# Three generations of edge buckets, adjacency counts in four pieces, and a GpSimd memset in front of each placing write

## The chip, the cores and the metric

The kernel runs on one core of one Trainium2 chip. The metric is the device time of one execution in microseconds; lower is better. A run executes the whole program once, from the inputs in HBM to the output in HBM.

## What is computed

Four graph layers are applied in turn to 6250 nodes of 64 features, with 200000 edges that are sorted by their destination `dst`. Cut to what matters here:

```
h = relu(layernorm(x)); x = x + relu(segment_sum(H_all[src, rel] * a, dst))       # L0: a message per edge
h = relu(layernorm(x)); x = x + A @ relu(A @ h)                                   # L1: two sums over edges
h = relu(layernorm(x)); x = x + gcn4(h)                                           # L2: four more sums with the same A, dense layers between
h = relu(layernorm(x))
v_e = segment_sum(edge_attr_48, src) / max(segment_sum(1, src), 1)                # L3: means of 48 edge features by src
x = x + relu(relu([h, v_e, u] @ W1 + b1) @ W2 + b2) @ W3 + b3
```

`A[dst, src]` counts the edges between two nodes. L3 sums by `src`, for which the edges are not sorted.

## The kernel before

The program has four stages, and every engine has its own hand-written list of instructions; what orders them between engines is semaphores only. There is no scheduler.

**The loop.** The edges are walked in 391 groups of 16 destination nodes (`NG`). GpSimd (POOL) gathers the rows of a table for the messages, four indirect DMAs for a group (L712, 1564 in all), up to 13 groups ahead. VectorE (DVE) makes one-hot matrices (L1395, L1369), TensorE multiplies them into a strip of `A` (L1860, L1861) and sums the messages (L1865). ScalarE (ACT) turns the strip into bytes (`store_counts`, L801 and L802 into `count_stage`), measures an overflow (L804, L805), and stores it with a DMA (L808) to `adjacency` in HBM; it waits for that store to land before it fills the single staging buffer again (`counts_stored`). Even and odd source tiles lie apart, `HW` = 100 words in each of two rows. Beside this the DVE and TensorE work out, for each edge, its place in `l3_sorted`: the edge's bucket (49 buckets of 128 source nodes) and its rank in it. Edges come in blocks of 4096 (`SB`, 48 blocks and a rest), and the bucket of an edge has a place in one of `GENS` = 2 **generations**: blocks 0 to 41 (`FIRST` = 42) go to the first with room for 30 x 128 rows in a bucket, the rest to the second with room for 6 x 128 (`CAPC`).

**The placing writes.** An edge's 48 features are split into three bf16 parts that add up exactly, 146 values in a row, and an indirect DMA of GpSimd writes 128 such rows to their places, 32 DMAs for a block. Two early blocks are placed right behind the last gather (L720, 64 writes); the others follow in one straight list, three row buffers (`rows16`) in turn (L738, 1499 writes). Each block waits once, on `l3_split`, for ScalarE to have finished its rows. A block's rows are made in three **steps**, high, middle and low (`split_high`, `split_middle`, `split_low`; ACT copies at L870, L857, L858, L881, DVE subtractions at L1272); `split_high` waits until the buffer's block before has landed (`l3_moved`). `split_step` puts the steps in slots of the ACT and DVE lists by `step_slot`: 120 of 135 steps (`AGG_STEPS`) over the 156 slots of the six aggregations, 15 over the 49 buckets of the first generation's sums.

**Six aggregations** (`agg`) compute `A @ U`. Each walks the 391 groups in 13 parts of 32 groups (`NH`, `HG`) and loads a part in two halves of 1600 KB (`half`, L578), each into its own buffer, and TensorE multiplies 25 and 24 tiles of a half (`multiply`, L1948); a half is loaded again once its tiles are done (`half_mm`). Between aggregation 3 and 4, and between 5 and 6, stand a dense layer (L1993 to L2004) and the scaling of `U` (L1288 to L1305), with no steps in them.

**The sums of L3.** Behind the last aggregation, for each generation and bucket, SyncE loads the bucket (L616), DVE and ACT make one-hot matrices (`node_hots`: L1681 and ACT L995, L997 in the first generation, L1684 in the second), and TensorE sums (`node_sums`, L2066). The sums of a generation start once its blocks have landed. The final MLP runs between the buckets of the last generation, four buckets behind.

Helper: `ch.link(ins)` lets the instruction raise a semaphore of its own engine and has the next instruction of that engine wait for it.

## Time and profile before

| | us |
|---|---|
| median of 3 runs (lowest to highest) | 4442.24 (4441.61 to 4444.57) |
| the profiled execution | 4443.71 |
| its span in the profile | 4442.0 |
| granted TensorE clock, mean | 0.837 of full speed |

All durations in the rows below are of the profiled execution. Its own time is 1.7 us above its span, and 1.5 us above the median, so a sum made in the span is carried over by adding 1.7 us. The engine named PE is TensorE, DVE VectorE, ACT ScalarE, POOL GpSimd and SP SyncE; a "q" behind a name is that engine's sequencer, which issues DMAs and handles semaphores. The row of a POOL indirect DMA (DMA_INDIRECT) covers the making of its descriptors on GpSimd, not the movement of the data.

### The profile page before, as it was taken

What the parts mean: (1) busy time and instruction counts of PE and PEld (TensorE: products, weight loads), DVE (VectorE), ACT (ScalarE), POOL (GpSimd) and SP (SyncE); (2) the same over time, 40 slices, a digit from 0 to 9 for tenths busy, and PEclk for the clock granted to TensorE, in tenths of its full rate; (3) what the DMA queues carried; (4) which work ended last, traced back from release to release, by engine and by line L of the source; (5) the groups of instructions that cost most, each with busy time, mean ns of one, the idle gap of its engine ahead of it and who ended that gap; (6) DMA issues with size and microseconds to landing.
All of it is one profiled execution on the core that took longest, in us unless ns stands there. A gap on an engine that the chain in (4) does not pass through costs nothing.

```text
span 4442.0 us, 78060 instructions
## 1 busy us (share of the span) xinstructions
PE 2917.6 (66%) x18243; PEld 1666.8 (38%) x18244; DVE 2719.6 (61%) x9781; ACT 1518.2 (34%) x3741; POOL 3060.2 (69%) x3186
## 2 busy tenths in 40 slices
PE   4477777777777777777807676185685775672556
PEld 2144444444444444444403333032332333331544
DVE  5488888898988889888852221511413213218878
ACT  2234444444444444434412221122122121133881
POOL 2277777777777777777777777777567776577650
PEclk8699998898998999989858888597597885885779
DMA  5554444444444444444327766286086670673664
GB/s 180 155 128 104 109 103 101 108 105 103 106 110 100 104 109 108 102 105 109 72 89 235 241 207 219 68 267 200 20 266 201 208 254 26 207 227 134 236 216 116
DMA packets 599825, 650.57 MB, mean 146 GB/s; under 512 B 422854, under 2 KB 435892, under 8 KB 593429
## 3 DMA queue, kind: packets, MB, share of 16 engines
q1 hardware_dynamic: 382453, 463.07, 34.0%
q0 software_dynamic: 100064, 110.65, 12.2%
q10 hardware_dynamic: 117184, 75.50, 5.8%
q8 instruction: 41, 0.67, 0.1%
q14 instruction: 83, 0.68, 0.1%
HBM read 453.58 MB, written 192.06 MB: 145 GB/s over the span
## 4 chain that ended last, share of the span: by engine, by line
POOL 26%; issue 10%; DVE 6%; PE 5%; DMA 3%; ACT 1%; DVEq 0%; POOLq 0%; ACTq 0%; SPq 0%
POOL l_sorted L738 25%; POOL l_sorted L720 1%; DVE hid_T L1681 1%; DMA ld_all<-l_sorted 1%; PE bank L2066 1%; PE bank L1998 1%; PE bank L2004 1%; PE bank L1948 1%; DMA rel_and_z<-adjacency 1%; DVE hid_T L1684 0%; ACT work L947 0%; DVE G L1549 0%; DMA rel_and_z<-l_sorted 0%; DVE G L1585 0%; PE bank L2038 0%
## 5 line engine op out<-in xcount | busy, mean ns | idle before, releaser
L738 POOL DMA_INDIRECT l_sorted<-arena,l_pos x1499 | 1466.2, 978 | 585.3 <-issue 454.6
L712 POOL DMA_INDIRECT ld_all<-rel_table,rel_and_z x1564 | 1493.5, 955 | 507.4 <-issue 409.6
L1860 PE MATMUL bank<-hid_T 128*128 128x400 f16 x2346 | 852.4, 364 | 494.6 <-DVE arena L1404 415.6
L1861 PE MATMUL bank<-hid_T 128*128 128x384 f16 x2346 | 835.3, 356 | 0.0
L1395 DVE TENSOR_SCALAR hid_T<-count_key,hid_T 128x400 f16<-128x400 int16 x2346 | 624.5, 334 | 17.0 <-PE bank L1865 10.6
L1948 PE MATMUL bank<-ld_all 128*128 128x512 fp8e4 (+1 forms) x1950 | 465.2, 401 | 186.4 <-DMA ld_all<-adjacency 113.2
L801 ACT CAST ld_all<-bank 128x400 fp8e4<-128x400 f32 x391 | 192.3, 492 | 1072.6 <-DMA adjacency<-ld_all 798.0
L1860 PEld LDWEIGHTS bank<-hid_T 128*128 x2346 | 240.0, 102 | 733.6 <-issue 579.6
L1948 PE MATMUL bank<-rel_and_z,ld_all 128*128 128x512 fp8e4 (+1 forms) x1872 | 417.5, 382 | 92.4 <-DMA rel_and_z<-adjacency 92.3
L1865 PE MATMUL bank<-ld_all,arena 128*32 x4692 | 428.7, 233 | 0.0
L1865 PEld LDWEIGHTS bank<-ld_all,arena 128*32 128x32 f32 x4692 | 319.7, 113 | 172.1 <-issue 127.9
L1369 DVE TENSOR_SCALAR hid_T<-io,arena 128x256 f16<-128x256 f16 x1564 | 360.3, 304 | 0.1
L1321 DVE COPY accT<-bank 128x512 f32<-128x512 f32 (+1 forms) x78 | 51.2, 656 | 503.8 <-PE bank L1948 503.8
L1948 PEld LDWEIGHTS bank<-ld_all 128*128 128x128 f16 x1950 | 194.7, 106 | 433.1 <-issue 270.0
L1948 PEld LDWEIGHTS bank<-rel_and_z,ld_all 128*128 128x128 f16 x1872 | 179.4, 101 | 326.4 <-issue 147.8
L1861 PEld LDWEIGHTS bank<-hid_T 128*128 x2346 | 241.9, 103 | 136.0 <-issue 52.1
L916 ACT COPY G<-bank 128x256 f32<-128x256 f32 (+1 forms) x78 | 27.9, 358 | 623.8 <-PE bank L1957 622.2
L2066 PE MATMUL bank<-ld_all,hid_T 128*128 128x145 bf16 x1188 | 117.3, 270 | 185.3 <-ACT hid_T L997 87.9
L804 ACT ACTIVATE ld_all<-bank,minus_max 128x400 f16<-128x400 f32 x391 | 238.2, 609 | 0.0
L805 ACT ACTIVATE ld_all<-bank,minus_max 128x384 f16<-128x384 f32 x391 | 231.1, 591 | 0.0
L802 ACT CAST ld_all<-bank 128x384 fp8e4<-128x384 f32 x391 | 189.6, 485 | 0.0
L1272 DVE TENSOR_TENSOR src_f<-src_f,bank 128x512 f32<-128x512 f32 x96 | 60.2, 682 | 211.4 <-ACT arena L858 211.3
(309 smaller groups left out, 4233.6 us busy)
## 6 DMA issues: line engine op xcount, KB each, us to landing
ld_all<-adjacency SPq DMA_DIRECT2D x72, 1600.0 KB
rel_and_z<-adjacency SPq DMA_DIRECT2D x72, 1600.0 KB, 9.5
l_sorted<-zeros SPq DMA_DIRECT2D x151, 424.0 KB
arena<-in_edge_attr SPq DMA_DIRECT2D x195, 256.0 KB
adjacency<-ld_all ACTq DMA_DIRECT2D x391, 100.0 KB
ld_all<-l_sorted SPq DMA_DIRECT2D x33, 1095.0 KB, 6.6
rel_table<-ld_all SPq DMA_DIRECT2D x49, 520.0 KB, 3.6
ld_all<-rel_table,rel_and_z POOLq DMA_INDIRECT x1564
```

The source lines that it names most:

```text
L712: pool.indirect_dma_start(ring[:, c % RING, 0:TW], None, rel_table, bass.IndirectOffsetOnAxis(ap=rel_i[:, c:c + 1], axis=0)).then_inc(s(f" ...
L738: pool.indirect_dma_start(l3_sorted, bass.IndirectOffsetOnAxis(ap=l3_pos[0:parts, n * SB_K + k:n * SB_K + k + 1], axis=0), rows16[q][0:par ...
L801: act.copy(count_stage[:, 0:w0], b0[:, 0:w0], saturate=False)
L802: act.copy(count_stage[:, w0:GW], b1[:, 0:GW - w0], saturate=False)
L804: act.activation(over_junk[:, 0:w0], b0[:, 0:w0], ACT.Relu, bias=minus_max[:], accum_out=over[:, bass.ds(g * 2, 1)])
L805: act.activation(over_junk[:, w0:GW], b1[:, 0:GW - w0], ACT.Relu, bias=minus_max[:], accum_out=over[:, bass.ds(g * 2 + 1, 1)]).then_inc(s( ...
L1369: v.tensor_scalar(lo_ring[:, q * K + k, :], io256[:], lo_in[:, k0 + k:k0 + k + 1], None, ALU.is_equal)
L1395: v.tensor_scalar(pair_hot[q % 2][:, k, :], count_key[:], pair_in[q % 2][:, k:k + 1], None, ALU.is_equal)
L1860: pe.matmul(b0[:, 0:w0], low[:, 0:P], pair_hot[q % 2][:, k, 0:w0], start=k == 0, stop=k == CG - 1)
L1861: pe.matmul(b1[:, 0:GW - w0], low[:, P:2 * P], pair_hot[q % 2][:, k, 0:GW - w0], start=k == 0, stop=k == CG - 1)
L1865: ins = pe.matmul(half_sums[q // 4][:, q % 4 * TW:(q % 4 + 1) * TW], weights[q % 2][:, k, :], ring[:, bass.ds((first64 + k) % RING, 1), 1: ...
L1948: ins = pe.matmul(bank[slot][:, 0:n * GN].rearrange("p (g d) -> p g d", d=GN), x16[:, t, :], a_half[side][:, 0:n, t // 2 * GN:(t // 2 + 1) ...
```

## The change

**Generations.** `GENS` becomes 3: blocks 0 to 35, 36 to 43 and the rest, with room for 26, 7 and 4 x 128 rows in a bucket. `l3_first` and `leave` become arrays over the generations that are past. The 135 steps are spread anew: 102 over the aggregations, 25 over the sums of generation 0, 8 over those of generation 1 (`STAGE_STEPS`), none in the last. The room for sorted rows grows from 36 to 37 x 128 rows a bucket, so 157 DMAs clear it instead of 152.

**Counts in four pieces.** A group's strip is stored as four rows of `QW` = 52 words (13 tiles, the last a tile short) instead of two of 100, so a store has 512 runs of 208 bytes instead of 256 runs of 400 bytes. In the aggregations each half is loaded as two pieces of 832 KB with a buffer and a semaphore of its own, and is asked for again once the 13 or 12 tiles of that piece are done. The order of tiles (even, then odd) and the number of matmuls stay. TensorE waits per piece.

**The memset.** Behind the loop, each of the 1499 placing writes gets a linked memset of 128 x 16 float32 in front: it clears a corner of `w_rel`, which nothing reads at that time, and the DMA waits for it. The two early blocks and the gathers have none.

**Small things.** `starts` is loaded into the buffer where it is used, one memset less; two semaphore pairs of paths that this input doesn't take become one; `packed_ready` is counted on `setup`.

```diff
-GENS = 2
-CAPC = (30, 6)
-FIRST = 42
-AGG_STEPS = 120
+GEN_END = (36, 44, NSB + 1)
+GENS = 3
+CAPC = (26, 7, 4)
+AGG_STEPS = 102
+STAGE_STEPS = (25, 8)
-HW = HI * GN // 4
+QT = -(-HI // 2)
+QW = QT * GN // 4
+PIECE_TILES = [(side, u0, min(u0 + QT, HI - side)) for side in range(2) for u0 in (0, QT)]
...
     for k in range(SB_K if n < NSB else REST_DMAS):
         parts = REST_TAIL if n == NSB and k == REST_K else P
+        ch.link(pool.memset(w_rel[:, 0:1, 0:16], 0))
         pool.indirect_dma_start(l3_sorted, bass.IndirectOffsetOnAxis(ap=l3_pos[0:parts, n * SB_K + k:n * SB_K + k + 1], axis=0),
                                 rows16[q][0:parts, k, :], None).then_inc(s(f"l3_moved{q}"), 16)
...
-                act.dma_start(adjacency_row[:, bass.ds(b, 1), q, :, :], count_words.rearrange("p (a o f) -> p a o f", a=1, o=2)).then_inc(s("counts_stored"), 16)
+                act.dma_start(adjacency_row[:, m, c, q, :, :], count_words.rearrange("p (a o f) -> p a o f", a=1, o=4)).then_inc(s("counts_stored"), 16)
...
-                        link(v.scalar_tensor_tensor(l3_first[:], held_out, leave[:, bass.ds(n, 1)], l3_first[:], ALU.mult, ALU.add))
+                        for g in range(GENS - 1):
+                            past = v.scalar_tensor_tensor(l3_past[:, g, :], held_out, leave[:, g, bass.ds(n, 1)], l3_past[:, g, :], ALU.mult, ALU.add)
+                        link(past)
...
-                    coming = [(m, side, 2 * (NH * a + m) + side + 1) for m in range(0 if a == 0 else 1, NH) for side in range(2)]
+                    coming = [(m, i, 4 * (NH * a + m) + i + 1) for m in range(0 if a == 0 else 1, NH) for i in range(4)]
...
-                        for side in range(2):
-                            pe.wait_ge(s(f"half_in{side}"), loads)
+                        for i, (side, u0, u1) in enumerate(PIECE_TILES):
+                            pe.wait_ge(s(f"piece_in{i}"), loads)
```

GpSimd at the start of the placing writes of the first block behind the loop, before (L738 is the write):

```order
L726 TENSOR_LOAD flags [waits flag2_ready]
L726 ISA x2
L727 COMPARE_AND_BRANCH
L738 DMA l_sorted<-arena,l_pos 242176x146 [waits l3_moved0,l3_pos_ready,l3_split]
L738 DMA l_sorted<-arena,l_pos 242176x146 x31
```

and of the changed kernel (L743 is the memset, L744 the write):

```order
L731 TENSOR_LOAD flags [waits flag2_ready]
L731 ISA x2
L732 COMPARE_AND_BRANCH
L743 MEMSET w_rel 128x16 [waits l3_moved0,l3_pos_ready,l3_split]
L744 DMA l_sorted<-arena,l_pos 248448x146 [waits pool_chain]
L743 MEMSET w_rel 128x16
L744 DMA l_sorted<-arena,l_pos 248448x146 [waits pool_chain]
```

The block's wait moved to the memset, and each write, which followed its predecessor with no wait of its own, now waits for the memset in front of it.

ScalarE in the sums of the first generation, before; L995 and L997 are the one-hot matrices of a bucket, L857, L858, L881 and L886 are parts of steps:

```order
L995 ACTIVATE hid_T<-io,node_key 128x128 x8
L997 ACTIVATE hid_T<-hid_T,ones 128x1152 [waits act_chain]
L857 CAST bank<-src_f 128x512 [waits split_less]
L857 CAST bank<-src_f 128x512 x2
L858 COPY arena<-src_f 128x32x48
L995 ACTIVATE hid_T<-io,node_key 128x128 [waits node_key,node_mm]
L995 ACTIVATE hid_T<-io,node_key 128x128 x8
L997 ACTIVATE hid_T<-hid_T,ones 128x1152 [waits act_chain]
L995 ACTIVATE hid_T<-io,node_key 128x128 [waits node_key,node_mm]
L995 ACTIVATE hid_T<-io,node_key 128x128 x8
L997 ACTIVATE hid_T<-hid_T,ones 128x1152 [waits act_chain]
```

and of the changed kernel at the same place:

```order
L1002 ACTIVATE hid_T<-io,node_key 128x128 x8
L1004 ACTIVATE hid_T<-hid_T,ones 128x1152 [waits act_chain]
L864 CAST bank<-src_f 128x512 [waits split_less]
L864 CAST bank<-src_f 128x512 x2
L865 COPY arena<-src_f 128x32x48
L1002 ACTIVATE hid_T<-io,node_key 128x128 [waits node_key,node_mm]
L1002 ACTIVATE hid_T<-io,node_key 128x128 x8
L1004 ACTIVATE hid_T<-hid_T,ones 128x1152 [waits act_chain]
L888 COPY arena<-src_f 128x32x48 [waits split_less]
L893 DMA src_f<-in_edge_attr 128x1536 [waits l3_split]
```

The low step (L881, now L888) that finishes a block stood three buckets behind the middle one; now it stands one bucket behind it.

## Rows read from the trace of the kernel before

**Rows 1.** The page's head and its first part, the busy time of each engine.

```profile
span 4442.0 us, 78060 instructions
PE 2917.6 (66%) x18243; PEld 1666.8 (38%) x18244; DVE 2719.6 (61%) x9781; ACT 1518.2 (34%) x3741; POOL 3060.2 (69%) x3186
```

**Rows 2.** GpSimd in order of time: start, duration, instruction, idle before it, releaser.

```profile
201.95 1.15 POOL L712 DMA_INDIRECT ld_all<-rel_table,rel_and_z  x1 [3.38 <-issue]
...
2198.56 0.95 POOL L712 DMA_INDIRECT ld_all<-rel_table,rel_and_z  x1 [0.30 <-issue]
...
2281.82 0.97 POOL L720 DMA_INDIRECT l_sorted<-ld_all,l_pos  x1 [0.30 <-issue]
2283.10 0.96 POOL L738 DMA_INDIRECT l_sorted<-arena,l_pos  x1 [0.30 <-issue]
...
4333.40 0.90 POOL L738 DMA_INDIRECT l_sorted<-arena,l_pos  x1 [0.30 <-issue]
```

**Rows 3.** GpSimd's waits behind the loop, 2283 to 4340 us: total, times, longest.

```profile
POOL l_sorted L738 <- issue: 454.6, 1491, 0.5
POOL l_sorted L738 <- ACT arena L881: 130.7, 8, 44.1
```

**Rows 4.** GpSimd in order of time: writes that wait between aggregations and in the sums.

```profile
3229.53 0.96 POOL L738 DMA_INDIRECT l_sorted<-arena,l_pos  x1 [44.13 <-ACT arena L881]
...
3799.84 0.96 POOL L738 DMA_INDIRECT l_sorted<-arena,l_pos  x1 [36.70 <-ACT arena L881]
...
4300.06 0.97 POOL L738 DMA_INDIRECT l_sorted<-arena,l_pos  x1 [13.14 <-ACT arena L881]
```

**Rows 5.** GpSimd in order of time, in setup: linked instructions one behind the other.

```profile
2.43 0.20 POOL L641 MEMSET ones<- 128x128 f32 x1
2.70 0.10 POOL L642 MEMSET minus_max<- 128x1 f32 x1
2.86 0.47 POOL L643 IOTA count_key<- 128x400 int16 x1
```

**Rows 6.** The same view: two memsets without links, and one form beside VectorE.

```profile
0.32 0.10 POOL L2103 MEMSET const-float32-0.0<- 128x1 f32 x1 [0.32 <-issue]
0.35 0.10 POOL L2103 MEMSET const-float32-1.0<- 128x1 f32 x1
...
35.52 0.94 POOL L688 MEMSET h<- 128x16 bf16 x1 [28.24 <-DMA h<-in_edge_attr]
...
65.03 0.17 POOL L688 MEMSET h<- 128x16 bf16 x1 [19.95 <-DMA h<-in_edge_attr]
```

**Rows 7.** ScalarE in order of time: the copy that releases the write at 4300.06 (rows 4).

```profile
4297.77 1.47 ACT L881 COPY arena<-dst_f 128x1536 bf16<-128x1536 bf16 x1 [1.48 <-DVE dst_f L1272]
```

**Rows 8.** Busy time of PE, PEld, DVE, ACT and POOL, 2283 to 4337 us.

```profile
2283.00:4337.00 2054.00, 1223.96 (x6264) 663.18 (x6264) 729.92 (x2344) 601.58 (x1085) 1466.17 (x1499) 0.78 0.58 188
```

**Rows 9.** VectorE's groups in the sums of generation 0, 4070 to 4300 us.

```profile
L1693 DVE TENSOR_REDUCE U<-bank 128x48 f32<-128x144 f32 x42 | 12.7, 303 | 31.3 <-PE bank L2066 31.3
```

**Rows 10.** The tail, 4337 to 4442 us: busy times, then VectorE's first groups.

```profile
4337.00:4442.00 105.00, 72.03 (x493) 46.18 (x493) 90.18 (x250) 21.00 (x39) 0.00 (x0) 0.92 0.49 120
L1684 DVE TENSOR_TENSOR hid_T<-io,ld_all 128x768 bf16<-128x768 f16 x33 | 31.3, 950 | 11.9 <-DMA ld_all<-l_sorted 11.8
L1684 DVE TENSOR_TENSOR hid_T<-io,rel_and_z 128x768 bf16<-128x768 f16 x16 | 15.2, 950 | 0.0
```

**Rows 11.** TensorE's groups, 2330 to 4005 us: count, busy us, mean ns, idle before.

```profile
L1948 PE MATMUL bank<-ld_all 128*128 128x512 fp8e4 (+1 forms) x1950 | 465.2, 401 | 186.4 <-DMA ld_all<-adjacency 113.2 <-DVEq L1306 73.2
L1948 PE MATMUL bank<-rel_and_z,ld_all 128*128 128x512 fp8e4 (+1 forms) x1872 | 417.5, 382 | 92.4 <-DMA rel_and_z<-adjacency 92.3
```

**Rows 12.** ScalarE in order of time, in the loop: a strip's cast and its store.

```profile
1018.24 0.38 ACTq L808 DMA_DIRECT2D adjacency<-ld_all  x1
1020.24 0.49 ACT L801 CAST ld_all<-bank 128x400 fp8e4<-128x400 f32 x1 [2.16 <-DMA adjacency<-ld_all]
1022.43 0.38 ACTq L808 DMA_DIRECT2D adjacency<-ld_all  x1
```

More of the change, by code:

```diff
@@ L259, in step_slot @@
                 return step * (2 * NH * 6) // AGG_STEPS
-            return 2 * NH * 6 + (step - AGG_STEPS) * NBK // (split_steps - AGG_STEPS)
+            step, slot = step - AGG_STEPS, 2 * NH * 6
+            for n in STAGE_STEPS:
+                if step < n:
+                    return slot + step * NBK // n
+                step, slot = step - n, slot + NBK
         step_at = {step_slot(step): step for step in range(split_steps)}
-        assert AGG_STEPS % 3 == 0 and len(step_at) == split_steps and FIRST <= AGG_STEPS // 3 + EARLY
+        assert AGG_STEPS % 3 == 0 and len(step_at) == split_steps == AGG_STEPS + sum(STAGE_STEPS) and len(STAGE_STEPS) == GENS - 1
+        assert all(GEN_END[g] <= (AGG_STEPS + sum(STAGE_STEPS[0:g])) // 3 + EARLY for g in range(GENS - 1))
         n_cols = (NSB + 1) * SB_K
@@ L998, in _ @@
                     split_step(2 * NH * 6 + t, (0, 1, 2))
-                act.wait_ge(s("node_hot"), NBK + 1)
+                for t in range((GENS - 2) * NBK):
+                    split_step(2 * NH * 6 + NBK + t, (0, 1, 2))
+                act.wait_ge(s("node_hot"), (GENS - 1) * NBK + 1)
                 for t in range(NBK):
@@ L1044, in _ @@
             link(v.memset(eps[:], EPS))
[L1045 to L1046 removed]
+            for g in range(GENS - 1):
+                v.memset(stay[:, GEN_END[g] - 1:GEN_END[g]], 0)
+                v.memset(leave[:, g, GEN_END[g] - 1:GEN_END[g]], 1.0)
             v.memset(s12[:, SRC_T:NT, :], 0)
@@ L1167, in _ @@
             link(v.tensor_scalar(l3_bucket, low_f, 1.0 / P, None, ALU.mult))
-            link(v.tensor_scalar(l3_pos[:, 0:FIRST * SB_K], l3_bucket[:, 0:FIRST * SB_K], float(CAP[0]), None, ALU.mult))
-            link(v.tensor_scalar(l3_pos[:, FIRST * SB_K:n_cols], l3_bucket[:, FIRST * SB_K:n_cols], float(CAP[1]), float(NBK * CAP[0]), ALU.mult, ALU.add))
+            for g in range(GENS):
+                of_gen = slice(((0,) + GEN_END)[g] * SB_K, GEN_END[g] * SB_K)
+                link(v.tensor_scalar(l3_pos[:, of_gen], l3_bucket[:, of_gen], float(CAP[g]), float(NBK * sum(CAP[0:g])), ALU.mult, ALU.add))
             v.wait_ge(s("setup_mm"), 2)
@@ L1347, in _ @@
                 chains.append(fast)
-                link(v.memset(digits[:, NG:WORDS * PACK], 0))
-                link(v.tensor_copy(digits[:, 0:NG], starts[0:1, 0:NG]))
+                link(v.tensor_copy(digits, starts))
                 link(v.scalar_tensor_tensor(digits[:, 0:NG], minus_base[0:1, :], float(K) / GN, digits[:, 0:NG], ALU.mult, ALU.add))
@@ L1434, in positions @@
                     v.tensor_tensor(l3_pos[:, cols], l3_pos[:, cols], l3_rank[:], ALU.add).then_inc(s("l3_pos_ready"), 1)
-                link(v.memset(count_words[:, GW // 4:2 * HW], 0))
+                link(v.memset(count_words, 0))
                 v.wait_ge(s("setup_mm"), 3)
@@ L2068, in node_sums @@
                     ins.then_inc(s("node_mm"), 1)
+                for n in range((GENS - 1) * NBK):
+                    node_sums(n // NBK, n)
                 for t in range(NBK):
-                    node_sums(0, t)
-                for t in range(NBK):
-                    node_sums(1, NBK + t)
+                    node_sums(GENS - 1, (GENS - 1) * NBK + t)
                     b = t // BT - 1
```

122 lines of the change are left out of this document (61 added, 61 removed).

## The prediction

> **What bounds the kernel now.** I first looked for the engine that never rests. The page's busy shares don't name it: GpSimd is busiest with 69%, TensorE has 66%, VectorE 61% [rows 1]. GpSimd in order of time does. Its gathers run from 201.95 to 2198.56 us, 1564 of them, one every 1996.6 / 1563 = 1.277 us, with an idle time of 0.30 us between two; the early writes follow at the same pace, and the 1499 later ones start at 2283.10 and end at 4333.40 + 0.90 = 4334.3 us [rows 2]. The gap of 0.30 is put down to "issue", that is, to no other engine. Behind the loop GpSimd waits for others only 8 times, 130.7 us in all, always for the copy that finishes a block's rows [rows 3]. So the time is 2283.1, plus 1498 starts at a pace, plus 130.7 of waits, plus a tail from 4334.3 to 4442.0, which is 107.7. The pace is (4333.40 - 2283.10 - 130.7) / 1498 = **1.281 us a write**.
>
> Two of the waits, 44.1 and 36.7, lie in the dense layers, where no steps stand; the other six, 130.7 - 80.8 = 49.9 us, lie in the sums of generation 0 [rows 3, 4]. At a dense layer GpSimd has two finished blocks, 64 writes or 82 us, and needs the third after 82 + 44.1 = 126.1 us, at the other layer after 118.7.
>
> **The memset.** It stands on this engine 1499 times, and each write waits for it. I call what it adds to the pace m. No row shows a write behind a memset, so I bound m by three neighbours.
>
> In setup, linked instructions stand one behind the other: 128x128 at 2.43, the next at 2.70, the next at 2.86. A linked memset thus costs its own 0.20 or 0.10 and 0.06 to 0.07 for the link [rows 5]. For 16 columns I take 0.10 + 0.10 x 15/127 = 0.11, with the link **m = 0.18**. It counts once if the write's gap of 0.30 stays as it is.
>
> The floor is no cost: two memsets without a link start 0.03 us apart [rows 6], and if the memset ran inside the gap of 0.30, m would be 0.
>
> The ceiling is a write that starts from rest. The copy that releases the write at 4300.06 ends at 4297.77 + 1.47 = 4299.24, so from permission to start pass 0.82 us [rows 4, 7], not 0.30. Part of these 0.82 is hidden today under the write before. If a write that waits for its memset has to go through all of it, the gap is 0.07 + 0.11 + 0.82 = 1.00 instead of 0.30, and m = 0.70. In that row, however, the engine's sequencer stood in front of a semaphore instruction with the write behind it not yet taken in, whereas now the memset and the write can both be taken in while the previous write runs. That, and that a link costs 0.06 in setup, is why I take the low neighbour.
>
> The Trainium skill's page "Perfetto Trace Analysis", section "DMA Instruction — SWDGE (GPSIMD)", has such an instruction decoded and pushed into a wait queue before its semaphores are looked at. That speaks for 0.18, and no row here shows it for a waiting write.
>
> m applies 1498 times and is partly given back at the dense layers, since two blocks then last 64m longer: waits there become 80.8 - 128 x 0.18 = 57.8. Net 1498 x 0.18 - 23.0 = **+246.6 us**.
>
> **What the memset meets on VectorE.** One form of memset takes 0.17 us at one time and 0.94 at another [rows 6]. The Trainium skill's page "SBUF — State Buffer", section "SBUF: two separate sides", says that GpSimd is locked out of a shared port pair while VectorE runs certain instructions; if every VectorE instruction did that, the sum would be the third rival's. The writes argue against much of it: 1466.17 / 1499 = 0.978 us on average with VectorE busy for 729.92 of 2054 us [rows 8], against 0.96 or 0.97 undisturbed [rows 2]. I add nothing.
>
> **Three generations, the steps.** In the sums of generation 0 the steps came too slowly: 42 buckets in 230 us are 5.5 us each [rows 9], three steps of 15 in 49 slots are 9.8 buckets or 54 us for a block, against 32 x 1.281 = 41 us of writes. With 25 steps it is 5.9 buckets or 32 us, and a block of writes lasts 32 x 1.461 = 47. GpSimd isn't starved there any more: **-49.9 us**. In generation 1, 8 steps in 49 slots are 18.4 buckets for a block, by the tail's 105 / 49 = 2.1 us [rows 10] 39 us, still under 47. In the aggregations 3 steps of 102 in 156 slots are 4.6 slots for a block; TensorE's matmuls and their waits for loads make (465.2 + 417.5 + 113.2 + 92.3) / 156 = 7.0 us a slot [rows 11], 32 us a block, under 47 too. Where steps stand next to the dense layers the tables agree: the last step before is in slot 76, the next in 78 and 79, in both kernels, so these two waits stay but for m.
>
> **The tail.** Once the last write lands, only the last generation is left. VectorE is busy for 90.2 of 105 us there, with one hot instruction of 0.950 us for 6 tiles in each of 49 buckets [rows 10]. With 4 tiles two thirds stay, about 0.65: 49 x 0.3 = **-15 us**. Generations 0 and 1 are done by then: generation 1 may start 4 blocks and a rest before the end, over 155 writes or 226 us, and needs about 49 x 2.1 = 103.
>
> **Counts in four pieces: nothing.** TensorE's matmuls wait 113.2 + 92.3 us for adjacency loads between 2330 and 4005 [rows 11], and smaller pieces should take much of that away. But the aggregations are paced by GpSimd: every step waits for a landed block, and TensorE, faster, waits longer for the copies between. What was saved goes into waiting for steps.
>
> In the loop the store gets 512 runs instead of 256. ScalarE's round is 2.19 us from cast to store and 2.00 from store to the next cast, 4.19 in all [rows 12], against 4 x 1.277 = 5.11 for GpSimd's four gathers, the cover that hides it. The added part is between 0 and 2.00, a doubling; 0.92 fit. I take 0 on the path. One VectorE instruction more for 8 groups, about 0.2 us in 41, and five more clearing DMAs are under the same cover; a memset less at `starts` is worth 0.
>
> **Sum.** 4443.7 + 246.6 - 49.9 - 15 = **4625 us**, of the profiled execution's own time, which stands 1.5 above the median. By pieces: 2283.1 + 1498 x 1.461 + 0.9 + 57.8 + 92.7 + 1.7. It is 4.1% slower. The other edits are worth 64.9 together, so the memset decides the sign: at m = 64.9 / 1370 = 0.047 us it comes out even.
>
> **Rivals.**
> - *The memset is free* (m about 0): it runs in the 0.30 us gap, which may be the wait of descriptor making alone. Then 4443.7 - 64.9 = **4379 us**, faster by 1.5%. For it: the gap is always 0.30 whatever stands around, and unlinked memsets cost 0.03. Against it: the change makes the write wait for the memset's end, and links cost 0.06 to 0.07 beside the memset itself. It decides below m = 0.047.
> - *Each write starts from rest* (m = 0.70): 2283.1 + 1498 x 1.981 + 0.9 + 92.7 + 1.7, with no wait left at the dense layers since 64 x 1.981 is above 126: **5346 us**. For it: the only row of a write that starts after a wait shows 0.82. Against it: the sequencer's reading ahead.
> - *VectorE holds up the memset*: 0.94 - 0.17 = 0.77 more in 36% of cases, m = 0.46: 2283.1 + 1498 x 1.741 + 0.9 + 22 + 92.7 + 1.7 = **5008 us**. Against it: the 0.978 above.
> - *The store becomes the loop's bound*: a doubling of 2.00 makes ScalarE's round 6.19, 391 x 1.08 = +422 us: **5047**. It decides once the store adds 0.92. For it: one buffer only, and ScalarE waits for nearly every store. Against it: the store's start and landing don't scale with its runs.
>
> **Chances.** The sum 0.44 (m from 0.1 to 0.35); from rest 0.22; VectorE or something between 0.10; the store 0.06; free 0.14; about even 0.04. The likeliest gives 4625. Leaving out only the cases of m below 0.1, the range is **4560 to 5350**, 0.82 of the chances; the likeliest case alone would span 4560 to 4800. A measurement of this kernel tells about 0.2% from no change. Faster by more 0.14, within 0.03, slower by more 0.83.
>
> **What the profile after would show.** Rows of a 128x16 memset of about 0.11 us between writes, and starts of writes 1.46 us apart (1.28 if it is free, 1.98 if each starts from rest). The first of them still at 2283 us; later if the store binds, with ScalarE's wait behind a store over 2.9 us. Two waits of some 34 and 25 us for the low step's copy and none in the sums. Waits of TensorE for adjacency much shorter, and no gain from it. A tail of 93 us behind GpSimd's last write. The forecast is wrong if writes are paced differently, or if GpSimd waits for more than two blocks.

## The result, and the profile after

| | us |
|---|---|
| predicted | 4625 (range 4560 to 5350) |
| changed kernel, median of 4 runs (lowest to highest) | 4581.18 (4573.49 to 4595.54) |
| kernel before, median of 4 runs beside it | 4442.95 (4441.61 to 4444.57) |
| ratio after to before, 95% interval | 1.0309 (1.0297 to 1.0321) |
| the profiled execution of the changed kernel, and its span | 4575.16, 4573.4 |

The changed kernel is 3.1% slower. The forecast had the side and, within 1%, the time; several terms of its sum are off, partly against each other. The sections below take these terms one by one.

In the changed kernel L743 is the memset, L744 the placing write, L888 the low step's copy (L881 before). The head of the page, its busy times, and four of its costliest groups (line, engine, operation, names, shapes, count; busy us, mean ns of one; idle time before it and what ended most of it):

```profile
span 4573.4 us, 80273 instructions
PE 2895.2 (63%) x18292; PEld 1684.2 (37%) x18293; DVE 2766.6 (60%) x9833; ACT 1517.8 (33%) x3741; POOL 3268.7 (71%) x4685
...
L744 POOL DMA_INDIRECT l_sorted<-arena,l_pos x1499 | 1483.3, 990 | 439.9 <-POOL w_rel L743 410.4
...
L1962 PE MATMUL bank<-ld_all 128*128 128x512 fp8e4 (+1 forms) x1950 | 435.7, 384 | 76.3 <-DVEq L1317 74.1
...
L1962 PE MATMUL bank<-rel_and_z,ld_all 128*128 128x512 fp8e4 (+1 forms) x1872 | 394.2, 367 | 1.7 <-DMA rel_and_z<-adjacency 1.7
...
L743 POOL MEMSET w_rel<- 128x16 f32 x1499 | 190.6, 127 | 64.9 <-ACT arena L888 63.5
```

GpSimd is busy 208.5 us longer than in [rows 1], 190.6 of them memsets. TensorE's waits for adjacency loads, 113.2 and 92.3 us in [rows 11], are all but gone, 1.7 in the second group, and no time came of it.

GpSimd in order of time (start, duration, instruction, idle before it and releaser), at the same place as [rows 2], then at a waiting write as [rows 4], then beside VectorE in the sums of generation 1, and its last write:

```profile
2484.97 0.98 POOL L744 DMA_INDIRECT l_sorted<-arena,l_pos  x1 [0.28 <-POOL w_rel L743]
2485.94 0.12 POOL L743 MEMSET w_rel<- 128x16 f32 x1
2486.35 0.97 POOL L744 DMA_INDIRECT l_sorted<-arena,l_pos  x1 [0.28 <-POOL w_rel L743]
2487.32 0.12 POOL L743 MEMSET w_rel<- 128x16 f32 x1
2488.71 0.97 POOL L744 DMA_INDIRECT l_sorted<-arena,l_pos  x1 [1.26 <-issue]
...
3170.11 0.11 POOL L743 MEMSET w_rel<- 128x16 f32 x1 [34.62 <-ACT arena L888]
3170.80 0.97 POOL L744 DMA_INDIRECT l_sorted<-arena,l_pos  x1 [0.58 <-POOL w_rel L743]
...
4264.69 1.18 POOL L744 DMA_INDIRECT l_sorted<-arena,l_pos  x1 [0.28 <-POOL w_rel L743]
4265.88 0.12 POOL L743 MEMSET w_rel<- 128x16 f32 x1
4266.28 1.19 POOL L744 DMA_INDIRECT l_sorted<-arena,l_pos  x1 [0.28 <-POOL w_rel L743]
...
4462.90 0.91 POOL L744 DMA_INDIRECT l_sorted<-arena,l_pos  x1 [0.28 <-POOL w_rel L743]
```

Three things are to be seen. The memset starts the moment the write before it ends, and the write follows 0.28 us behind the memset, not 0.30: writes start **1.38 us apart**, not 1.46. One write, that at 2488.71, starts 1.26 us behind its memset instead of 0.28, and I call such a write late. And at 4265 a write takes 1.18 us instead of 0.97.

GpSimd's waits behind the loop, 2283 to 4600 us (total, times, longest), against [rows 3]:

```profile
POOL l_sorted L744 <- POOL w_rel L743: 410.4, 1476, 0.6
POOL w_rel L743 <- ACT arena L888: 63.5, 2, 34.6
POOL l_sorted L744 <- issue: 29.4, 23, 1.6
```

The two waits are those at the dense layers, 34.6 and 28.9; in the sums there is none. The last line is the late write of above: 23 times a write starts about 1 us late. These are the 50th write behind the loop, with a gap of 1.64 us, and from the 146th (the one at 2488.71) to the 1490th every 64th, each with 1.26.

The tail, from the end of the last write at 4463.8 (the columns are stretch, its length, busy time of PE, PEld, DVE, ACT and POOL, granted TensorE clock, DMA share, GB/s), with the stretch ahead of it, and two of VectorE's groups:

```profile
4370.00:4464.00 94.00, 1.61 (x12) 1.04 (x10) 1.65 (x5) 0.00 (x0) 74.17 (x135) 0.50 0.09 27
4464.00:4573.00 109.00, 73.97 (x395) 45.13 (x395) 78.08 (x251) 20.99 (x39) 0.00 (x0) 0.81 0.32 83
...
L1696 DVE TENSOR_TENSOR hid_T<-io,ld_all 128x512 bf16<-128x512 f16 x32 | 21.8, 683 | 0.0
...
L1708 DVE TENSOR_REDUCE hid_T<-bank 128x48 f32<-128x144 f32 x50 | 15.1, 303 | 8.8 <-PE bank L2081 8.8
```

Against [rows 10] VectorE has 12 us less to do (78.1 for 90.2), as forecast, its hot instruction takes 0.68 us for 0.95. But the tail is 4573.4 - 4463.8 = 109.6 us, where it was 107.7. TensorE has fewer matmuls (395 for 493) and is busy longer (74.0 for 72.0), because its granted clock is 0.81 where it was 0.92, and VectorE now waits for it 8.8 us at one line where [rows 10] had it busy for 86% of the tail.

### The profile page after: what moved, and what is told of

It reads as the page before. It is cut to its first block, busy times and chain, and to the rows that moved or that the text cites. A ratio compares the mean times of both kernels' runs of the same rounds, so it can differ in the third digit from the quotient of the medians.

```text
span 4573.4 us, 80273 instructions
## 1 busy us (share of the span) xinstructions
PE 2895.2 (63%) x18292; PEld 1684.2 (37%) x18293; DVE 2766.6 (60%) x9833; ACT 1517.8 (33%) x3741; POOL 3268.7 (71%) x4685
## 4 chain that ended last, share of the span: by engine, by line
POOL 35%; issue 9%; PE 4%; DVE 2%; ACT 1%; DMA 0%; DVEq 0%; POOLq 0%; ACTq 0%; SPq 0%
POOL l_sorted L744 30%; POOL w_rel L743 4%; POOL l_sorted L725 1%; PE bank L2013 1%; PE bank L2019 1%; ACT work L954 0%; PE bank L2059 0%; PE bank L2067 0%; PE bank L2053 0%; PE bank L1962 0%; DVE work L1299 0%; DVE hid_T L1696 0%; DVE work L1621 0%; DVE G L1561 0%; DVE G L1597 0%
## 5 line engine op out<-in xcount | busy, mean ns | idle before, releaser
L744 POOL DMA_INDIRECT l_sorted<-arena,l_pos x1499 | 1483.3, 990 | 439.9 <-POOL w_rel L743 410.4
L1962 PE MATMUL bank<-ld_all 128*128 128x512 fp8e4 (+1 forms) x1950 | 435.7, 384 | 76.3 <-DVEq L1317 74.1
L1962 PE MATMUL bank<-rel_and_z,ld_all 128*128 128x512 fp8e4 (+1 forms) x1872 | 394.2, 367 | 1.7 <-DMA rel_and_z<-adjacency 1.7
L2081 PE MATMUL bank<-ld_all,hid_T 128*128 128x145 bf16 x1217 | 139.6, 290 | 260.7 <-issue 118.3
L1962 PEld LDWEIGHTS bank<-ld_all 128*128 128x128 f16 x1950 | 193.2, 104 | 293.2 <-issue 110.8
L743 POOL MEMSET w_rel<- 128x16 f32 x1499 | 190.6, 127 | 64.9 <-ACT arena L888 63.5
L1972 PE MATMUL bank<-work,accT 128*128 128x64 f32 x588 | 86.6, 296 | 234.9 <-DVE accT L1332 234.9
L2081 PEld LDWEIGHTS bank<-ld_all,hid_T 128*128 128x128 bf16 x1217 | 119.9, 128 | 287.9 <-issue 287.7
```

The costliest lines, as they stand in the source:

```text
L743: ch.link(pool.memset(w_rel[:, 0:1, 0:16], 0))
L744: pool.indirect_dma_start(l3_sorted, bass.IndirectOffsetOnAxis(ap=l3_pos[0:parts, n * SB_K + k:n * SB_K + k + 1], axis=0), rows16[q][0:par ...
L1962: ins = pe.matmul(bank[slot][:, 0:n * GN].rearrange("p (g d) -> p g d", d=GN), x16[:, 2 * u + side, :], a_piece[i][:, 0:n, (u - u0) * GN:( ...
L2081: ins = pe.matmul(bank[n % 3][:, 0:KEY], node_hot[n % 2][:, k, :], sorted_in[n % 3][:, k, 0:KEY], start=k == 0, stop=k == CAPC[gen] - 1)
```

## Experiments

Each starts from the kernel that its text names and changes what the text says; the kernel before ran beside each on the same chip. A ratio is always to the kernel before. In the texts of what was expected, "hots" are one-hot matrices.

### The changed kernel without its memsets

```diff
-                        ch.link(pool.memset(w_rel[:, 0:1, 0:16], 0))
```

> The changed kernel with the 1499 memsets taken out; three generations, steps and four pieces stay. Theory A (the memset costs its own 0.12 us on the engine that bounds, the rest of the change is a gain): pace of the writes back to 1.28 us, no stall every 64 writes, no write waits in the sums; with start at 2284, two dense waits of 44 and 37 us and a tail of 93 to 108 us the time is 4380 to 4398 us. Rival B (the other edits gain nothing, because the matrices of generation 1 now hold up the writes beside them and the tail is no shorter): 4425 to 4445 us.

Measured: 4427.08 us (4419.31 to 4439.38), ratio 0.9960 (0.9946 to 0.9974). This is in rival B's range: all the other edits together win some 17 us of the median, not the 64.9 of the forecast. In its profiled execution (span 4437.6) the first write is at 2285.60, and GpSimd's last one ends at 4309.3, 25.0 us before that of the kernel before. The waits in the sums are gone, as forecast:

```profile
POOL l_sorted L743 <- issue: 455.4, 1494, 0.3
POOL l_sorted L743 <- ACT arena L887: 81.1, 5, 43.5
```

but the writes are 1.296 us apart in the mean, (4308.35 - 2285.60 - 81.1) / 1498, against 1.281, which is 22 us, and the tail is 4437.6 - 4309.3 = 128.3 us, 20.6 more than before. So two losses stand against what was to be gained, and neither comes from the memset. The experiments with tiles and with added matmuls take them up.

### The kernel before, with the memset alone

```diff
+                        ch.link(pool.memset(w_rel[:, 0:1, 0:16], 0))
                         pool.indirect_dma_start(l3_sorted, ...
```

> The kernel before with the linked memset in front of each of the 1499 later writes, nothing else. Theory A: pace 1.27 + 0.11 = 1.38 us undisturbed, 1498 x 0.11 = +165, 24 stalls of 1 us every 64 writes +24, given back 14 at the dense layers and about 18 in the sums of generation 0: 4443 + 157 = about 4600 us. Rival B (the memset's price depends on the three generations or the pieces, through VectorE): pace under 1.33 us undisturbed and under 4540 us.

Measured: 4585.62 us (4581.40 to 4587.57), ratio 1.0315 (1.0298 to 1.0333): as slow as the whole change. First and last write start at 2283.82 and 4474.10, and the waits for the copy are

```profile
POOL w_rel L738 <- ACT arena L882: 89.7, 6, 34.3
POOL l_sorted L739 <- issue: 29.4, 23, 1.6
```

so a write has (4474.10 - 2283.82 - 89.7) / 1498 = 1.402 us, 0.121 more than before. Of the 181 us that the memsets add, 41 are given back by shorter waits (130.7 to 89.7), 9 more than theory A said, which is most of why the time is below its 4600. The price hardly depends on the generations, 0.121 us a write with two and 1.411 - 1.296 = 0.115 with three, and the 23 late writes are there too, the same ones by number.

### A satisfied wait in place of the memset

```diff
-                        ch.link(pool.memset(w_rel[:, 0:1, 0:16], 0))
+                        pool.wait_ge(s("l3_split"), m + 1)
```

> The changed kernel with no memsets; instead each write waits on a semaphore that has long been reached. It separates the wait as such from the memset. If the stall every 64 writes comes from waits that keep the sequencer from reading ahead, it shows here too, every 64 or 128 writes. If a wait as such costs pace, the pace is over 1.30. Theory A: pace 1.28 us, no stalls, the time of the kernel without memsets within 10 us.

Measured (one run): 4424.59 us; 1.27 us from write to write in the median, 1.297 in the mean of the unbroken ones, as without memsets. A wait in front of each write that was satisfied long ago costs nothing that this run shows, and no write is late by 1 us.

### The memset kept, but the write doesn't wait for it

```diff
-                        ch.link(pool.memset(w_rel[:, 0:1, 0:16], 0))
+                        pool.wait_ge(ch.sem, ch.base + ch.k)
+                        ch.also(pool.memset(w_rel[:, 0:1, 0:16], 0))
```

Each memset waits for the memset before it, which is long done, and the write for nothing.

> The changed kernel with the same 1499 memsets, but the writes don't wait for them: only the next memset waits for the one before, which is long done. It separates the memset's own time from the link. Theory A (GpSimd's time of the memset counts, and the gap of 0.28 before a write is the write's own): pace 1.38 us as with the link, within 0.02. Rival: the link is what costs, and without it the memset goes into the gap: pace 1.28 to 1.31 us and the time near that of the kernel without memsets. The stall every 64 writes: gone if the waiting write keeps the sequencer from reading ahead, there if it goes by the count of instructions.

Measured (one run): 4448.19 us, 133 us less than the changed kernel. GpSimd in order of time:

```profile
2486.12 0.97 POOL L745 DMA_INDIRECT l_sorted<-arena,l_pos  x1 [0.18 <-issue]
2487.09 0.13 POOL L744 MEMSET w_rel<- 128x16 f32 x1
2487.40 0.98 POOL L745 DMA_INDIRECT l_sorted<-arena,l_pos  x1 [0.18 <-issue]
```

The same memsets stand there, just as long, and the writes start 1.28 us apart. The gap behind the write before is 0.13 + 0.18 = 0.31 us: the memset runs inside it. It isn't wholly free: over all writes the pace is (4318.87 - 2284.58 - 78.8) / 1498 = 1.305 us against 1.296 without memsets, some 14 us for 1499 of them, where the waited-for memset costs 172. So the gap isn't idle time that GpSimd needs behind a memset; it is a stretch of about 0.30 us behind the last write in which a memset is all but free, unless the next write waits for the memset. Then most of it, 0.28, begins anew at the memset's end. **The wait costs, not the work.** The late writes are absent here too.

### Two linked memsets

```diff
                         ch.link(pool.memset(w_rel[:, 0:1, 0:16], 0))
+                        ch.link(pool.memset(w_rel[:, 0:1, 16:32], 0))
```

> The changed kernel with a second linked memset of 128x16 ahead of each write. The forecast's own term, a linked memset costs its duration and a link of 0.06 us: the starts of writes go from 1.38 to some 1.56 us apart, no wait left at the dense layers that is longer than 25 us, time 4800 to 4850. Rival, only the first one is cheap and the second waits for the first from rest: 1.7 us or more, over 5000. On the delay of about 1 us that the changed kernel has at every 64th write: if it goes by instructions on GpSimd (every 128th), it comes at every 42nd or 43rd write now, some 35 times; if by writes, at every 64th as before, 23 times.

Measured: 4848.98 us, ratio 1.0904 (1.0883 to 1.0926).

```profile
2614.07 0.12 POOL L743 MEMSET w_rel<- 128x16 f32 x1
2614.25 0.11 POOL L744 MEMSET w_rel<- 128x16 f32 x1
2614.64 0.97 POOL L745 DMA_INDIRECT l_sorted<-arena,l_pos  x1 [0.28 <-POOL w_rel L744]
...
2617.16 0.12 POOL L743 MEMSET w_rel<- 128x16 f32 x1
2617.35 0.11 POOL L744 MEMSET w_rel<- 128x16 f32 x1
2618.72 0.97 POOL L745 DMA_INDIRECT l_sorted<-arena,l_pos  x1 [1.26 <-issue]
```

The second memset adds 0.17 us (1.55 between writes in the median), which is a memset and its link as in setup [rows 5]: 0.18 and 0.19 from memset to memset here. The first adds 0.10. So the forecast's 0.18 is right for a memset that stands behind a memset and too high for one that takes part of a write's gap. The late writes are still the 50th, 146th, 210th and so on: they go by writes, not by instructions, of which there are half as many again. What they wait for isn't settled. They appear only where a write waits for a memset of its own engine, in five of five such kernels, and in none of the others.

### The counts in four pieces alone

```diff
-GEN_END = (36, 44, NSB + 1)
-GENS = 3
-CAPC = (26, 7, 4)
-AGG_STEPS = 102
-STAGE_STEPS = (25, 8)
+GEN_END = (42, NSB + 1)
+GENS = 2
+CAPC = (30, 6)
+AGG_STEPS = 120
+STAGE_STEPS = (15,)
-                        ch.link(pool.memset(w_rel[:, 0:1, 0:16], 0))
```

> The kernel before with the counts in four pieces alone (two generations, 120 and 15 steps, no memset). The forecast's step, no worth on the path: 4443 within 5 us, although TensorE's waits for adjacency loads (113.2 + 92.3 us before) fall below 100. Rival, the gain reaches the path or the doubled runs of the store cost something: under 4430, or the first placing write later than 2286 us and the time over 4455.

Measured: 4444.93 us (4442.21 to 4450.08), ratio 0.9996 (0.9987 to 1.0005). The adjacency waits of [rows 11] vanish here as well:

```profile
L1961 PE MATMUL bank<-ld_all 128*128 128x512 fp8e4 (+1 forms) x1950 | 444.0, 389 | 74.5 <-DVEq L1316 72.9 <-DMA ld_all<-adjacency 1.6
L1961 PE MATMUL bank<-rel_and_z,ld_all 128*128 128x512 fp8e4 (+1 forms) x1872 | 395.5, 369 | 0.9 <-DMA rel_and_z<-adjacency 0.9
```

205 us of waiting on an engine that doesn't set the pace were worth nothing, and the store's doubled runs cost nothing on the path: the first write is at 2281.93. The store itself did get longer. Between 400 and 2190 us ScalarE's waits for it are 859.7 us for 321 here and 836.9 for 317 in the changed kernel, against 714.8 for 296 before, so one is 2.68, 2.64 and 2.41 us. The 0.2 to 0.3 us that it grew by are well under the 0.92 of the prediction.

### Generation 1's one-hot matrices in tiles, no memsets

On the kernel without memsets, generation 1's one-hot matrices are made as generation 0's are, a copy of the keys and one VectorE instruction for each 128x128 tile, instead of one instruction of 128x896.

```diff
-                    if gen == 0:
+                    if gen < GENS - 1:
...
-                        for k in range(CAPC[0] - ACT_HOTS):
+                        for k in range(CAPC[0] - ACT_HOTS if gen == 0 else CAPC[gen]):
```

> The changed kernel without its memsets, and generation 1's hot columns made by 7 instructions of 128x128 a bucket, as generation 0's are, instead of one of 128x896. Theory E, the one wide VectorE instruction is what stretches GpSimd's writes there (75 writes in 116 us instead of 91): the writes keep 1.28 us, the last one lands 15 to 20 us earlier, time some 4405 to 4412. Rival F, the writes are stretched by something else that runs in those 116 us (loads of 112 KB a bucket, the sums, any VectorE work): no more than 5 us are won, time 4420 to 4430.

Measured: 4414.64 us (4409.76 to 4418.47), ratio 0.9931 (0.9918 to 0.9945), by the ratios some 13 us less than without this edit. The median is 3 us above theory E's range and 5 below rival F's, so the time alone doesn't decide; the trace does. The groups of GpSimd and VectorE in generation 1's sums, first without the edit (4107 to 4223 us), then with it (4103 to 4225 us):

```profile
L743 POOL DMA_INDIRECT l_sorted<-arena,l_pos x75 | 93.6, 1249 | 22.9 <-issue 22.9
L1695 DVE TENSOR_TENSOR hid_T<-io,ld_all 128x896 bf16<-128x896 f16 x32 | 34.8, 1086 | 2.0 <-DMA ld_all<-l_sorted 1.5
L1695 DVE TENSOR_TENSOR hid_T<-io,rel_and_z 128x896 bf16<-128x896 f16 x16 | 17.4, 1087 | 2.0 <-DMA rel_and_z<-l_sorted 1.8
```

```profile
L743 POOL DMA_INDIRECT l_sorted<-arena,l_pos x96 | 93.3, 972 | 29.3 <-issue 29.3
L1692 DVE TENSOR_SCALAR hid_T<-io,node_key 128x128 bf16<-128x128 f16 x360 | 64.3, 277 | 1.8
```

VectorE has more to do with the tiles (64.3 us for 52.2), and yet the writes are back at 0.97 us, 96 of them in 122 us instead of 75 in 116. It is the wide instruction that stretches GpSimd's writes, up to 1.84 us for one. The kernel before ran this instruction only behind GpSimd's last write; the third generation put 49 of them beside it. The last write ends at 4286.5 for 4309.3; 20 of these 22.8 us are the pace.

Whether the form or the length of 1.09 us does it can be read from the trace of the kernel before, which has other VectorE instructions beside GpSimd's writes:

```profile
3726.33 0.69 DVE L1609 TENSOR_TENSOR work<-work,hid_T 128x512 f32<-128x512 f32 x1 [2.27 <-ACT work L947]
3726.43 1.43 POOL L738 DMA_INDIRECT l_sorted<-arena,l_pos  x1 [0.31 <-issue]
...
2860.00 5.39 DVE L1288 TENSOR_REDUCE work<-U 128x64 f32<-128x3136 f32 x1
2861.95 0.97 POOL L738 DMA_INDIRECT l_sorted<-arena,l_pos  x1 [0.30 <-issue]
```

An instruction of 0.69 us with two inputs in SBUF goes with a write of 1.43 us (the copy L1600, which follows it, leaves writes at 0.97 where it runs alone), and one of 5.39 us with a single input leaves the write at 0.97. The subtractions L1272 take 0.68 us and have two inputs too, but one of them lies in PSUM (`bank`): the writes beside them alone stay at 0.96 and 0.97, 154 of 154. Two-input instructions of 128x256 (0.42 us) go with writes of up to 1.23. So it isn't the length that decides; all 27 writes of over 1.10 us behind the loop stand beside a TENSOR_TENSOR whose two inputs both lie in SBUF. The rule isn't sharp: L1609 left other writes at 0.97, and beside one-input instructions of 128x256 writes took mostly 1.03 and once 1.10.

The Trainium skill's page "SBUF — State Buffer", section "SBUF: two separate sides", has a VectorE instruction with two SBUF inputs hold a port pair against GpSimd instructions that read SBUF, whichever of the two starts first, and the other fully blocked meanwhile. The direction fits: the 128x896 form reads two tensors, the tile form one and a column of keys, and the memset, which reads none, stays at 0.12 us beside it (0.125 in the mean of 77 in the changed kernel). The writes of that stretch are 0.28 us longer in the mean and 0.87 at most; no row shows the whole 1.09.

### TensorE kept busy ahead of the tail

On the kernel without memsets 640, on the changed kernel 760 added matmuls between the sums of generation 1 and those of the last generation, into a bank that nothing reads.

```diff
+                with pe.Fori(0, 80) as i:
+                    for k in range(8):
+                        pe.matmul(bank[7][:, 0:256], ident16[:], io256[:], start=True, stop=True)
                 for t in range(NBK):
                     node_sums(GENS - 1, (GENS - 1) * NBK + t)
```

> The changed kernel without its memsets, with 640 matmuls of 128x256 into an unused bank between the sums of generation 1 and those of the last (dummy work; results are the same). Theory C, the tail behind the last write is long because TensorE stands idle before it and then works at a granted clock of 0.5 to 0.6: the tail's clock comes to over 0.9, the tail falls from 128 us to 92 to 98, the time to 4392 to 4405. Rival D, the tail is set by VectorE, loads and the round between engines: the tail stays over 110 us whatever the clock, time 4415 to 4430.

> The changed kernel as it is, with 760 matmuls of 128x256 into an unused bank between the sums of generation 1 and those of the last. Theory C: the tail's clock goes from 0.81 to over 0.9, the tail from 109.6 to 92 to 98 us, the time to 4564 to 4570. Rival D: the tail stays at 107 to 110, time 4578 to 4585.

Measured: 4434.30 us (4427.87 to 4442.44), ratio 0.9973 (0.9962 to 0.9983), and 4593.10 us (4590.36 to 4599.50), ratio 1.0332 (1.0316 to 1.0348). Nothing is won; by the ratios 6 and 10 us are lost, but the intervals overlap with those without the added work. All the times of both theories were missed: 4434.30 is above rival D's 4430, 4593.10 above its 4585, and the changed kernel's tail became 126.3 us. The stretch of the added matmuls and the tail, for the kernel without memsets, and the end of that stretch by itself:

```profile
4223.00:4309.00 86.00, 69.86 (x632) 62.01 (x630) 0.77 (x2) 0.05 (x1) 62.32 (x65) 0.92 0.11 33
4309.00:4433.00 124.00, 100.18 (x395) 59.96 (x395) 78.01 (x250) 20.95 (x39) 0.00 (x0) 0.58 0.26 69
...
4280.00:4293.00 13.00, 12.86 (x118) 11.28 (x116) 0.00 (x0) 0.00 (x0) 9.95 (x11) 1.00 0.11 32
4293.00:4309.00 16.00, 0.00 (x0) 0.01 (x1) 0.77 (x2) 0.05 (x1) 9.08 (x10) 0.61 0.17 50
```

The added matmuls end at 4292.9, 12 us before the last write, and TensorE then stands idle for 16 us until the tail's first matmul at 4309.0. The clock was at 1.00 in their last 13 us, fell in that pause, and was at 0.58 over the tail. So this run doesn't answer theory C as it stands, since the full clock was lost before the tail began; work that runs into the tail without a pause wasn't tried. It shows that the added work ahead buys nothing if a pause of 16 us follows. The next experiment decides from the other side.

### Added matmuls inside the tail

On the kernel with tiles and no memsets, 2 and then 5 added matmuls behind each of the last generation's 49 sums.

```diff
                     ins.then_inc(s("node_mm"), 1)
+                    if gen == GENS - 1:
+                        for k in range(2):
+                            pe.matmul(bank[7][:, 0:256], ident16[:], io256[:], start=True, stop=True)
```

> The kernel of the run with generation 1's hots in tiles (no memsets), and behind each of the last generation's 49 sums 2 matmuls of 128x256 into an unused bank (dummy work; results are the same), so that TensorE has as many matmuls a bucket there as the kernel before. Theory G, the clock in the tail is low because TensorE's work in the tail itself became thinner with 4 tiles instead of 6: the granted clock rises from 0.64 to 0.9 or more, the tail falls from about 121.5 us to 95 to 105, the time to 4390 to 4402. Rival H, the density inside the tail doesn't matter: the clock stays between 0.5 and 0.8, 98 matmuls of 0.11 to 0.28 us come on top, the time is 4415 to 4440.

> As the run with 2 dummy matmuls a bucket in the tail, with 5 of them. Theory G: the clock is 0.95 or more through most of the tail, tail 95 to 105 us (5 x 49 matmuls of 0.11 us are 27 us, of which most lies in TensorE's idle time), time 4388 to 4402. Rival H: clock between 0.5 and 0.8 and 245 matmuls of 0.22 to 0.28 us on top, tail over 150 us, time over 4440.

Measured: 4390.18 us (4389.29 to 4392.47), ratio 0.9874 (0.9858 to 0.9891), and 4391.01 us (4390.63 to 4391.66), ratio 0.9875 (0.9858 to 0.9891). The tails without added matmuls, with 2, and with 5, and below the first two their first 40 us:

```profile
4287.00:4408.00 121.00, 90.51 (x395) 54.62 (x395) 78.48 (x251) 21.01 (x39) 0.00 (x0) 0.66 0.29 75
...
4287.00:4307.00 20.00, 12.42 (x54) 7.73 (x55) 13.05 (x43) 2.38 (x5) 0.00 (x0) 0.50 0.30 84
4307.00:4327.00 20.00, 17.88 (x66) 10.82 (x65) 12.75 (x41) 3.33 (x6) 0.00 (x0) 0.50 0.28 74
```

```profile
4286.00:4387.00 101.00, 74.95 (x493) 46.17 (x493) 77.93 (x251) 21.00 (x39) 0.00 (x0) 0.94 0.34 90
...
4286.00:4306.00 20.00, 12.95 (x82) 7.70 (x83) 15.51 (x51) 2.38 (x5) 0.00 (x0) 0.78 0.39 105
4306.00:4326.00 20.00, 16.46 (x119) 10.56 (x117) 17.17 (x58) 5.00 (x9) 0.00 (x0) 1.00 0.35 92
```

```profile
4286.00:4389.00 103.00, 89.63 (x640) 61.40 (x640) 78.09 (x251) 21.00 (x39) 0.40 (x1) 0.93 0.34 88
```

With 98 matmuls more TensorE is busy for 15.6 us less, and the kernel 24 us faster. Both kernels come to the tail with an idle TensorE and a clock of 0.50 in the 20 us before it; the one with more matmuls is at the full clock 20 us later, the other still at 0.50. So what keeps the clock low is how little TensorE does inside the tail, and not the pause ahead of it. The third generation thus had two effects on the tail: less work for VectorE, and for TensorE too, 395 matmuls instead of 493, with which it no longer held the full clock of 2.4 GHz but fell for much of the tail to the 1.2 of the other level. All tails side by side, by the profiled executions:

| kernel | matmuls in the tail | granted clock | tail, us |
|---|---|---|---|
| before | 493 | 0.91 | 107.7 |
| counts in four pieces alone | 493 | 0.87 | 110.5 |
| before with the memset | 493 | 0.87 | 110.8 |
| changed | 395 | 0.81 | 109.6 |
| satisfied wait, no memset | 395 | 0.69 | 118.9 |
| tiles, no memset | 395 | 0.66 | 121.5 |
| changed, TensorE busy ahead | 395 | 0.61 | 126.3 |
| memset not waited for | 395 | 0.59 | 126.6 |
| no memset | 395 | 0.58 | 128.3 |
| no memset, TensorE busy ahead | 395 | 0.58 | 128.5 |
| two linked memsets | 395 | 0.55 | 131.7 |
| tiles and 2 added | 493 | 0.94 | 101.7 |
| tiles and 5 added | 640 | 0.93 | 102.6 |
| changed, with tiles and 2 added | 493 | 0.94 | 102.3 |

Within each count of matmuls the tail follows the clock, and only the ones with more matmuls have a high one every time. The changed kernel's four runs spread over 22 us and the five without memsets over 20, where those with 2 or 5 matmuls added in the tail lie within 5. That this spread is the tail's clock is likely and not shown. Only the clock of the whole span is on record for every run: without memsets it is highest, 0.823, in the fastest run and lowest, 0.815, in the slowest, but in the changed kernel it doesn't order them (0.810 at 4575.16, 0.811 at 4595.54). The Trainium skill's page "TensorE: Matmul & The Clock Gate", section "Part 1: The HAM clock gate (the "warmup" mystery)", has the clock follow how busy the array has been of late, and puts the cost of the ramp below 1% for a typical kernel. The direction is as in these tails; here the clock was worth 20 us of 4410, 0.5%, and 16% of a tail of 121.5.

### The changed kernel with tiles and 2 added matmuls

The two edits of above on the changed kernel, memsets and all.

> The changed kernel with its memsets, with generation 1's hots in tiles and 2 dummy matmuls behind each of the last generation's sums. If the losses simply add up: 4463.8 for the end of the last write, less about 12.5 writes x 1.38 = 17 us that the wide hots cost in generation 1's sums, plus a tail of 101.7 and 1.7 around the span, is 4550 us, within 6. The tail's granted clock is over 0.9. Rival, the memset hides what the two mends win (GpSimd's writes stay stretched beside 7 narrow instructions a bucket, now that a memset stands between them): 4565 or more.

Measured: 4550.61 us (4548.84 to 4553.49), ratio 1.0237 (1.0220 to 1.0254). The last write starts at 4443.93, the tail is 4547.1 - 4444.8 = 102.3 us at a clock of 0.94, writes are 1.38 us apart and 23 are late by 1 us. The parts add up: 4550.61 - 4390.18 = 160.4 us is what the waited-for memset costs in a kernel in which neither of the two losses is left, after what shorter waits at the dense layers give back.

## The prediction, step by step

The sum and what took the place of each of its terms, for the profiled executions (spans 4442.0 and 4573.4):

| term | forecast | measured | from |
|---|---|---|---|
| start of the placing writes | 0 | +2.4 | 2285.54 against 2283.10; 2281.0 to 2285.7 in all kernels |
| memsets, 1498 m | +269.6 | +172 | 1.411 us a write in the changed kernel, 1.296 without memsets |
| writes beside the wide hots | 0 | +22 | 1.296 against 1.281, both without memsets; 20 of it go with the tiles |
| waits at dense layers | -23.0 | -17.3 | 63.5 against 80.8 |
| waits in the sums of generation 0 | -49.9 | -49.9 | none left |
| tail | -15 | +1.9 | 109.6 against 107.7 |
| counts in four pieces | 0 | 0 | ratio 0.9996 |
| sum | +181.7 | +131 | 131.4 by the spans |

The split between the second and third term is taken from the kernel without memsets. In the changed kernel itself the wide instructions cost less: with tiles and added matmuls its writes from the first to the last take 2161.9 us for 2177.4, with the same 63.5 us of waits, so 15.5 us go with the wide instructions. That leaves some 179 us for the memsets, close to the 181 of the kernel before with the memset.

**The bound: right.** GpSimd's writes set the time up to the tail, and the 205 us of waiting that TensorE lost came to nothing.

**The memset: the mechanism right, the size off.** The step that failed is "it counts once if the write's gap of 0.30 stays as it is" with m = 0.18. The gap became 0.28, and the 0.06 of a link doesn't come on top of it: 0.12 - 0.02 = 0.10 us. To this come 23 late writes of about 1 us, 0.016 us a write, which no row of before hinted at; together 0.115 to 0.121. By the prediction's own sign, "wrong if writes are paced differently", this step is wrong: 1.38 us apart, not 1.46. The rival of the free memset was nearer than its chance of 0.14 says: it is nearly true if the write doesn't wait (0.009 us a write), and the reason given against it, the wait, is what decides. The one row of a write from rest (0.82 us, [rows 4, 7]) has its like in the changed kernel: from the end of the copy, 3168.48 + 1.48 = 3169.96, to the write at 3170.80 are 0.84 us with a memset in between. So the price from rest is as it was read, and it isn't what a write pays behind a memset in the stream. That the reason is the sequencer's reading ahead, as the prediction argues, no run shows.

**VectorE: right for the memset, wrong for the writes.** "I add nothing" rested on writes of 0.978 us with VectorE busy for 36% of the time [rows 8]. But an average over 2054 us hides the form that matters: the writes with no VectorE instruction beside them take 0.967 us, so 0.011 x 1499 = 16 us of stretching were already in it, with single writes of up to 1.43 us beside two-input instructions. The change put 49 such instructions of 1.09 us beside GpSimd. The memset itself stayed at 0.12. The row that was to be read is the hot instruction of [rows 10], and the question is what runs beside it now.

**The steps: right,** down to the two waits left (34.6 and 28.9, where some 34 and 25 were forecast).

**The tail: the step failed.** "With 4 tiles two thirds stay", worth -15 us, holds for VectorE, which had 12 us less to do. It left out TensorE, which loses a third of its sums too and with them its clock: even when the clock is held, the tail is 101.7, 6 us less than before, and without it anything up to 131.7. VectorE was 86% busy there [rows 10], which I read as VectorE's tail; TensorE was 69% busy at nearly the full clock. At 0.58 of it the tail without memsets has TensorE busy for 100.2 us and VectorE for 78.8.

**Pieces and store: right,** both at zero on the path.

So a forecast within 1% was partly luck: the memset term was 98 us too high; 41 us of losses that it didn't see (2, 22 and 17) and 6 us of waits not given back stood on the other side, which leaves 4625 - 50 = 4575 for the profiled execution.

## What to carry to other kernels

A small instruction between two indirect DMAs of GpSimd was all but free here as long as the DMA didn't wait for it; if it does, the gap in front of the DMA begins anew, and 1499 of them cost 140 to 160 us. Before work is moved beside another engine's critical stretch, ask for each of its wide instructions what it does to that engine, and look at the form, not at the busy share; a row of the kernel before can already hold the answer. And when a change thins TensorE's work in a stretch, look at the granted clock there: two matmuls a bucket that compute nothing gave 24 us back. Of the whole change the three generations are worth keeping, with generation 1's one-hot matrices in tiles and the added matmuls: 4390.18 us, 1.3% below the kernel before, the fastest version measured. The four pieces are in it too and were worth nothing where they were tried alone.

## What the runs showed of the hardware

- A write of GpSimd that waits for a memset of its own engine starts 0.28 us after it, and every 64th such write 1.26 us after it, with one memset in front or two. In the nine kernels without such a wait no write is late. The cause is open.
- An indirect DMA's descriptors took 1.25 us in the mean and up to 1.84 instead of 0.97 beside a VectorE instruction of 128x896 with two inputs in SBUF, and 0.97 beside seven of 128x128 with one. In the kernel before, a one-input instruction of 5.39 us left them at 0.97, and a two-input one of 0.69 us goes with 1.43.
- TensorE's granted clock was 1.00 at the end of 72 us of unbroken matmuls, 0.50 again when the tail began 16 us later, and 0.58 over a tail of 395 matmuls in 124 us. In a tail of 493 matmuls in 101 us, which also began at 0.50, it was 0.94.
